# Gate projection of a Mamba chunk: one group of eight before the scan, or one group in each scan block

## The reference

```
def _mamba(h, Win, Wconv, bconv, Wx, Wdt, bdt, Alog, Dp, Wout):
    xz = h @ Win
    x, z = jnp.split(xz, 2, axis=-1)
    x = silu(causal_conv4(x, Wconv) + bconv)
    dbc = x @ Wx
    dt = jax.nn.softplus(dbc[..., :DT_RANK] @ Wdt + bdt)
    Bm = dbc[..., DT_RANK:DT_RANK + D_STATE]
    Cm = dbc[..., DT_RANK + D_STATE:]
    dA = exp(dt * -exp(Alog));  dBx = dt * Bm * x
    # scan over time:  hc = dA_t * hc + dBx_t ;  y_t = sum_n hc_n * C_t,n
    y = (y + Dp * x) * jax.nn.silu(z)
    return y @ Wout
```

## Time and profile before

| | |
|---|---|
| time before, median of 3 runs | 9859.0 us (9858.45 to 9881.77) |
| profiled execution, its own time | 9858.85 us |
| its span on the slowest core (core 6) | 9857.0 us, so 1.85 us lie around it |
| spans of the eight cores | 9832.6 to 9857.0 us |
| busy share of the span | DVE 49%, PE 45%, ACT 32%, POOL 2% |
| Mamba chunks | DBCC is copied in the first at 4828.6 us, in the last at 8731.3 us |

### The profile page before, as it was taken

The page is one execution under the profiler, slowest core; times in us unless marked ns, Lnnn a source line. Parts: engine busy times, 40 slices in busy tenths (PEclk is TensorE's granted clock), DMA queues, the critical chain, the costliest instruction groups (busy, mean ns, idle before and its releaser), DMA issues.

```text
span 9857.0 us, 59735 instructions; the slowest of 8 cores (9832.6 to 9857.0 us)
## 1 busy us (share of the span) xinstructions
PE 4388.2 (45%) x12160; PEld 1344.7 (14%) x12160; DVE 4828.5 (49%) x8072; ACT 3130.5 (32%) x4401; POOL 172.6 (2%) x221
## 2 busy tenths in 40 slices
PE   3645564556456588983323222232323222232325
PEld 1211111111112133330100000000000000000112
DVE  2343334334433321225475766757475766757553
ACT  3323322332232221113342424343342424333312
POOL 0000000000000000000000000000000000000000
PEclk8866666666667796665555555555555555555556
DMA  1133472100001132100000000000000000000001
GB/s 43 12 29 35 54 80 24 17 0 4 4 0 9 58 129 87 52 18 0 19 2 20 1 12 9 8 14 4 19 2 20 1 13 9 7 15 4 1 26 43
DMA packets 203015, 223.07 MB, mean 23 GB/s; under 512 B 131441, under 2 KB 140049, under 8 KB 200561
## 3 DMA queue, kind: packets, MB, share of 16 engines
q0 software_dynamic: 141104, 76.50, 7.3%
q1 hardware_dynamic: 61570, 142.76, 4.4%
HBM read 278.07 MB, written 65.03 MB: 35 GB/s over the span
## 4 chain that ended last, share of the span: by engine, by line
DVE 38%; PE 30%; ACT 14%; issue 13%; DMA 3%; DVEq 1%; POOL 0%; ACTq 0%; SPq 0%; POOLq 0%
DVE HBF L1682 12%; PE P2U L199 8%; PE PSU L199 6%; DVE DBXP L1678 4%; PE P3U L199 4%; PE PSU L845 3%; PE PSU L854 3%; DVE SROW L814 2%; DVE XCC L1424 1%; DVE SCBW L873 1%; DVEq L35 1%; ACT DAP L1637 1%; DVE CARRY L1687 1%; DMA WINZ<-wmsc 1%; ACT SCBW L881 1%
## 5 line engine op out<-in xcount | busy, mean ns | idle before, releaser
L1663 PE MATMUL P3U<-DBXP,EYEB 128*128 128x512 bf16 x1024 | 598.1, 584 | 2231.6 <-DVE DBXP L1689 2231.6
L1682 DVE TENSOR_TENSOR_SCAN HBF<-DAP,CARRY,DBXP 128x512 bf16<-128x512 bf16 x1024 | 1314.6, 1284 | 108.2 <-DVE DBXP L1678 2.3
L1649 ACT ACTIVATE DAP<-DT_CH,ACOL 128x512 bf16<-128x512 bf16 x768 | 549.1, 721 | 840.9 <-DVE HBF L1682 837.5
L873 DVE CAST SCBW<-PSU 128x512 bf16<-128x512 f32 x512 | 354.1, 692 | 773.2 <-PE PSU L845 767.7
L1678 DVE TENSOR_TENSOR DBXP<-U_CH,BREP 128x512 bf16<-128x512 bf16 x1024 | 429.8, 420 | 399.3 <-ACT DAP L1637 299.9
L854 PE MATMUL PSU<-SCBW,HV 128*64 128x512 bf16 x960 | 459.1, 478 | 162.9 <-DVE SCBW L873 123.0
L845 PE MATMUL PSU<-QCB,RCB 128*128 128x512 bf16 x1024 | 473.9, 472 | 66.5 <-DVE ATTO L887 53.4
L1663 PEld LDWEIGHTS P3U<-DBXP,EYEB 128*128 128x128 bf16 x1024 | 106.7, 104 | 2746.4 <-issue 2746.4
L881 ACT CAST SCBW<-PSU 128x512 bf16<-128x512 f32 x512 | 300.1, 586 | 568.6 <-PE PSU L845 566.0
L199 PE MATMUL P2U<-YLN,W1E 128*128 128x256 bf16 x1024 | 465.7, 631 | 15.4 <-DMA W2E<-wfsc 15.4
L1689 DVE TENSOR_TENSOR DBXP<-HBF,CREP 128x512 bf16<-128x512 bf16 x1024 | 424.8, 415 | 1.6 <-issue 1.6
(11 more groups left out here) (324 smaller groups left out, 7317.1 us busy)
## 6 DMA issues: line engine op xcount, KB each, us to landing
wfsc<-L_ffn_w POOLq DMA_DIRECT2D x16, 2048.0 KB, 90.9
SW1H<-wfsc SPq DMA_DIRECT2D x64, 256.0 KB, 2.7
SW3H<-wfsc SPq DMA_DIRECT2D x64, 256.0 KB, 3.0
SW2C<-wfsc SPq DMA_DIRECT2D x32, 512.0 KB, 3.7
W1E<-wfsc SPq DMA_DIRECT2D x8, 2048.0 KB, 7.8
W2E<-wfsc SPq DMA_DIRECT2D x8, 2048.0 KB, 12.4
WINS<-wmsc SPq DMA_DIRECT2D x64, 256.0 KB, 2.6
WINZ<-wmsc SPq DMA_DIRECT2D x64, 256.0 KB, 2.7
```

Source lines behind the costliest of these rows:

```text
L873: b.sV.inc(v.tensor_copy(SCBW[kt % 2][:], PSU[kt % 2][:, :]))
L1649: b.sS.inc(s.activation(DAP[ni % 2][:], DT_CH[:, dt * QC:(dt + 1) * QC], AF.Exp, scale=acol))
L1663: b.sT.inc(t.matmul(ybank[:, :], EYEB[:], DBXP[ni % 2][:], start=(ni == 0), stop=(ni == 7)))
L1682: b.sV.inc(v.tensor_tensor_scan(HBF[ni % 2][:], DAP[ni % 2][:], DBXP[ni % 2][:], CARRY[:, dt * 16 + n: dt * 16 + n + 1], ALU.mult, ALU.add))
```

## The change

The z stage is taken out as a stage. Its eight matmul groups, weight loads and Silus are spread over the eight blocks of pass 0. The first two weight loads are issued after the first two `emit_dtmm` of the chunk; the load of dt + 2 waits for the group of dt. In block dt of pass 0, PE runs the z group of dt behind the matmul of `emit_dtmm(dt + 2)` and ahead of the eight identity matmuls; ACT takes its Silu behind the block's last Exp and ahead of the copy of the y bank. A constant column with -pi is also written once, and nothing reads it.

```
@@ stage 2 of each chunk
-                    def _zs_g(g, dr=dr, zw_m=zw_m, zt_m=zt_m):
-                        for dt in range(KT):
-                            if dt >= 2:
-                                b.sT.wait(g, zt_m[dt - 2])
-                            else:
-                                b.sT.wait(g)
-                            zw_m[dt] = [ydma(g, WINZ[dt % 2][:], ...
-                    def _zs_t(t, c0=c0, zw_m=zw_m, zs_b=zs_b):
-                        for dt in range(KT):
-                            wait_marks(t, zw_m[dt])
-                            if dt >= 2:
-                                b.sS.wait(t, zs_b + dt - 1)
-                            else:
-                                b.sV.wait(t)
-                            b.sT.inc(mm_group(t, PSU[4 + dt % 2][:, :], ...
-                    def _zs_s(s, zt_m=zt_m):
-                        for dt in range(KT):
-                            b.sT.wait(s, zt_m[dt])
-                            b.sS.inc(s.activation(ZSB[:, dt * QC:(dt + 1) * QC],
-                                                  PSU[4 + dt % 2][:, :], AF.Silu))
@@ pass 0, behind emit_dtmm(0), emit_dtmm(1), the softplus of 0 and 1
+                            def _zw0(g, dr=dr):
+                                b.sT.wait(g)
+                                for j in (0, 1):
+                                    zw_m[j] = [ydma(g, WINZ[j][:], ...
+                            b.y(_zw0)
@@ each block dt of a pass
-                            tb_y = b.sT.n
+                            tb_y = b.sT.n + (1 if npass == 0 else 0)
...
-                            def _blk_t(t, npass=npass, dt=dt):
+                            def _blk_t(t, npass=npass, dt=dt, c0=c0, vb_cap=vb_cap):
+                                if npass == 0:
+                                    wait_marks(t, zw_m[dt])
+                                    if dt >= 2:
+                                        b.sS.wait(t, zsilu_m[dt - 2])
+                                    else:
+                                        b.sV.wait(t, vb_cap)
+                                    b.sT.inc(mm_group(t, PSU[4 + dt % 2][:, :],
+                                             [(WINZ[dt % 2][:, kt * 128:(kt + 1) * 128],
+                                               mv_h(kt, c0, QC)) for kt in range(KT)]))
+                                    zt_m[dt] = b.sT.n
                                 ybank = PSU[dt % 2]
...
+                            if npass == 0 and dt + 2 < KT:
+                                def _zwn(g, dt=dt, dr=dr):
+                                    b.sT.wait(g, zt_m[dt])
+                                    zw_m[dt + 2] = [ydma(g, WINZ[dt % 2][:], ...
+                                b.y(_zwn)
+                            if npass == 0:
+                                def _zsl(s, dt=dt):
+                                    b.sT.wait(s, zt_m[dt])
+                                    b.sS.inc(s.activation(ZSB[:, dt * QC:(dt + 1) * QC],
+                                                          PSU[4 + dt % 2][:, :], AF.Silu))
+                                    zsilu_m[dt] = b.sS.n
+                                b.s(_zsl)
```

More of the change, by code:

```diff
@@ L129, in build_program @@
         C_EPS, C_MAGIC, C_HALFPI, C_TINY = (CONST[:, i:i + 1] for i in range(4))
+        C_NEGPI = CONST[:, 5:6]
         SROW = est.enter_context(nc.sbuf_tensor("SROW", [1, 2 * T], F32))
@@ L233, in _c_v @@
                 v.memset(CONST[:, 2:3], PI / 2)
+                v.memset(CONST[:, 5:6], -PI)
                 b.sV.inc(v.memset(CONST[:, 3:4], 1e-12))
@@ L1443, in emit_dir @@
                     b.s(_s1_s)
-                    zt_m, zw_m = {}, {}
-                    zs_b = b.sS.n
-                    zs_tb = b.sT.n
-                    for dt in range(KT):
-                        zt_m[dt] = zs_tb + dt + 1
-                    def _zs_g(g, dr=dr, zw_m=zw_m, zt_m=zt_m):
-                        for dt in range(KT):
-                            if dt >= 2:
-                                b.sT.wait(g, zt_m[dt - 2])
-                            else:
-                                b.sT.wait(g)
[L1457 to L1460, removed]
-                    def _zs_t(t, c0=c0, zw_m=zw_m, zs_b=zs_b):
-                        for dt in range(KT):
-                            wait_marks(t, zw_m[dt])
-                            if dt >= 2:
-                                b.sS.wait(t, zs_b + dt - 1)
-                            else:
-                                b.sV.wait(t)
[L1469 to L1472, removed]
-                    def _zs_s(s, zt_m=zt_m):
-                        for dt in range(KT):
-                            b.sT.wait(s, zt_m[dt])
-                            b.sS.inc(s.activation(ZSB[:, dt * QC:(dt + 1) * QC],
-                                                  PSU[4 + dt % 2][:, :], AF.Silu))
-                    b.s(_zs_s)
                     def _dbc_s(s):
@@ L1541, in emit_dtphv @@
                         b.v(_v)
+                    zw_m, zt_m, zsilu_m = {}, {}, {}
                     for npass in range(2):
@@ L1550, in emit_dir @@
                             emit_softplus(1)
+                            def _zw0(g, dr=dr):
+                                b.sT.wait(g)
+                                for j in (0, 1):
+                                    zw_m[j] = [ydma(g, WINZ[j][:],
+                                                    hbm_ap(WSC[dr], 1048576 + j * 131072,
+                                                           [[1024, 128], [128, 8], [1, 128]]))]
+                            b.y(_zw0)
                         rp_gm = {}
@@ L1665, in emit_dir @@
                             b.t(_blk_t)
+                            if npass == 0 and dt + 2 < KT:
+                                def _zwn(g, dt=dt, dr=dr):
+                                    b.sT.wait(g, zt_m[dt])
+                                    zw_m[dt + 2] = [ydma(g, WINZ[dt % 2][:],
+                                                         hbm_ap(WSC[dr],
+                                                                1048576 + (dt + 2) * 131072,
+                                                                [[1024, 128], [128, 8], [1, 128]]))]
+                                b.y(_zwn)
[6 more added lines that the diff above has]
+                                b.s(_zsl)
                             if has_pv:
```

## The result

The changed kernel takes 9667.9 us (median of 9 runs, 9664.0 to 9739.6) against 9867.4 us of the kernel before in the same comparisons (10 runs). The ratio of the two is 0.9799, 95% interval 0.977 to 0.9827: about 198 us less, or 171 to 227 us by the interval. The forecast was 9662 us, 196.6 us less than the profiled execution before. Three of the nine executions (9698.2, 9710.6 and 9739.6 us) lie above the forecast range of 9640 to 9695 us.

A forecast was written before the change was run, and what follows sets the result against it. No engine is busy half the span; the z stage was taken to lie on the chain in all eight chunks. 9858.85 minus 196.6 us, with moved work costing 0, gave 9662 us, range 9640 to 9695.

The forecast's parts named there:

- What goes: Gap in each chunk from last dbc matmul to the DBCC copy's table load: 202.0 us in eight, 5.4 stay, 196.6 go.
- the shift of what comes behind DBCC: Matmuls of dt, softplus and staging of B and C shift with the DBCC copy; nothing new is late.
- What is added: Z work moved into the 64 blocks of pass 0, on TensorE, ScalarE and DMAs: cost 0, hidden in idle time.
- TensorE: Z group ahead of a block's identity matmuls takes 3.6 us with 2.5 us to spare; cost 0.
- the bound of 9.1 us: In a pass 0 block, a z group must last about 9.1 us (3.6 + 2.5 + 3.0) to hold DVE.
- ScalarE: Silu and table load, 1.88 us a block, fit ACT's 5.21 us wait before the y bank copy; 3.3 us left, cost 0.
- DMAs: The same 64 loads of 256 KB move from the gap into blocks; no DVE slowdown taken, at most 166 us.
- ScalarE as the bound: Silu and its load in each pass 0 block are paid in full, 120 us: 9782 us; chance 0.05.
- More gained: Loads ahead of the DBCC copy go too (10 us), or block clock rises (up to 19 us): 9633 to 9652; chance 0.04.
- the wait was covered: Staging or direction parameters hold the softplus anyway, so the time stays 9859 us; chance 0.03.
- The slower rival: Z group delays identity matmuls, DVE and y bank: 230 us, 9892 us; decides from 3.07 us a block; chance 0.03.

The follow-up runs named there:

- e1: Changed kernel without any z work (weight loads, groups, Silus), ZSB set to a constant by memset; Mamba stage 4256.3 us, +1.5 against the changed kernel.
- e2: Changed kernel with the z group behind the block's eight identity matmuls instead of ahead; Mamba stage 4590.1 us, +335.3 against the changed kernel.
- e4: Changed kernel with the Silu of z and the y bank copy in one piece of code; Mamba stage 4172.2 us, -82.6 against the changed kernel.
- e6: Changed kernel with the Silu run twice in each block of pass 0; Mamba stage 4252.9 us, -1.9 against the changed kernel.
- e9: Changed kernel with each z group run six times over in pass 0; Mamba stage 4445.5 us, +190.7 against the changed kernel.
- e10: Kernel before, with only ACT's copy to DBCC moved ahead of the z stage; Mamba stage 4429.3 us, -15.9 against the kernel before.
- e3: Changed kernel with the Silu run four times in each block of pass 0; Mamba stage 4420.4 us, +165.6 against the changed kernel.
- e7: Changed kernel with each z group run three times over in pass 0; Mamba stage 4255.0 us, +0.2 against the changed kernel.
- e11: Changed kernel with ScalarE's block work in one piece and pass 1's gate product written into YSB instead of DBXP0; 9373.9 us, ratio to before 0.9476.
- e5: Changed kernel with ScalarE's block work, except Silu, in one piece opened by a tiny Ln; Mamba stage 4009.8 us, -245.0 against the changed kernel.

## Why the prediction was right

**What goes.** On core 6 the eight gaps fell from 202.0 to 5.4 us by the same reading, the 196.6 us of the sum. The whole stage lost 191.6 us there, so 5.0 us came back elsewhere. A part of it is a step that the sum valued at nothing, the shift of what comes behind DBCC. In the kernel before, the z stage left PE at the high clock for the matmuls of dt; the second chunk, before and after:

```profile
5384.94 0.58 ACT L1483 CAST DBCC<-P3U 64x512 bf16<-64x512 f32 x1
5385.77 0.64 PE L199 MATMUL P3U<-DBCC,WDTB 32*128 32x512 bf16 x2 [2.83 <-ACT DBCC L1483]
...
5386.28 1.28 ACT L1515 ACT_TABLE_LOAD   x1 [0.76 <-PE P3U L199]
```

```profile
5310.94 0.58 ACT L1449 CAST DBCC<-P3U 64x512 bf16<-64x512 f32 x1
5311.76 1.01 PE L200 MATMUL P3U<-DBCC,WDTB 32*128 32x512 bf16 x2 [2.20 <-ACT DBCC L1449]
...
5312.48 1.28 ACT L1481 ACT_TABLE_LOAD   x1 [0.96 <-PE P3U L200]
```

Two matmuls take 0.64 us there and 1.01 us here, and ACT goes on 1.34 us behind the start of the copy there and 1.54 us here: 0.2 us a chunk, 1.6 us at most. The granted clock is 1.00 from 5385 to 5387 us before, and 0.50 from 5311 to 5313 us after. From the copy to the first copy of a y bank the eight chunks took 382.4 us before and 383.6 us after, and 383.7 us in e1, which has no z group there. Another 2.9 us came in pass 1, whose code did not change (from the first to the last gate of each chunk 1352.3 and 1355.2 us). The kernels with z work in the blocks and this pass 1 (e2 to e4, e6 to e9) have 1354 to 1355 us there; before, e1 and e10 have 1351 to 1352. The time lies in single gaps of 0.2 to 0.7 us on DVE, at a place that shifts from block to block: of the 56 stretches between two gates, 20 are longer than 24.25 us in the changed kernel and 14 in the one before. That is a pattern, and its cause stays open.

**What is added.** TensorE: 3.59 us against 3.6, with 2.65 us to spare against 2.5; the clock is 0.50 in most groups, and where it rose the group takes down to 2.92 us. e9 confirms the bound of 9.1 us, by its size and by the wait at which it shows. One reading behind the 3.6 us was wrong without effect: the first group of chunk 1 starts 4805.42 - 4802.51 = 2.91 us behind the load's issue, and the 2.67 us are the load's own. ScalarE: 3.33 us left against 3.3; e3 and e6 confirm it from both sides. DMAs: in pass 0 e1, without the loads, is within 0.1 us of the changed kernel, so they cost nothing there, and the scans stay at 1283 to 1287 ns.

**What was luck.** The mechanism and its terms are confirmed on the stage: 190.4 us against 196.6, with some 5 us that the sum had at nothing. That the median of the whole time lies within 6 us of the forecast says less, since the interval on the gain is 171 to 227 us and the kernel before came to 9867.4 us, not 9859.0.

**The rivals.** ScalarE as the bound is out by e6 and e1. More gained is out: the load ahead of the DBCC copy is still there, and the clock rose only for the end of some groups and the first identity matmul behind them (0.38 us in 19 blocks of core 6). The last identity matmul, where it would have paid, still takes 0.58 to 0.59 us in all 64. e4 shows, on the copy of the y bank, that a load goes when the two functions share a piece. That the wait was covered is out by the 8.17 us. The slower rival is out at 3.59 us; its mechanism is real, but shows only beyond 9 us (e9: 2.98 us a block, against the 3.07 from which it decides). The other order, e2, costs 5.24 us a block.

## What to carry to other kernels

Work that nobody near it needs, in a row on a chain, can move into another engine pair's idle times, and what it is worth there can be read before: the length of the gap from one profile, the room from the waits of the engines that take it. Where in the block it stands decides between free and dearer than before, since each engine works in its order. A wait that is removed pays only down to the next one that ends at the same place; look for it among the engines that read the same buffer.

## What the runs showed of the hardware

- A group of 24 matmuls crosses from 0.50 to 0.99 of the clock within itself and takes 7.3 us, twice the 3.59 us of 8 (e7 and the changed kernel). Idle time that is filled with more matmuls is filled at another rate.
- The stages ahead of Mamba, the same in all kernels but for the memsets, took 4707 to 4786 us over all profiled cores, and up to 52 us more on one core than on another of the same execution (e11, 4708 to 4760; in e2 one core has 4784 us at a mean clock of 0.604 and another 4737 us at 0.609). The Mamba stage of one execution agrees within 1 to 7 us over the eight cores. For a change in one stage, that stage's own span is by far the sharper measure.
- In the blocks of the Mamba stage each piece of ScalarE code begins with a load of 1.28 us. It is free in front of a long wait for data, if something that needs no data calls for it: in e5 the tiny Ln did this, for 0.20 us.
